# Moving the normalisation stage of the first network one step later in a software-pipelined two-network kernel

## What is computed

```python
h = jnp.maximum(_layernorm(x, axis=-1), 0.0)
x = x + _L0_gnn_ref(h, adj, L0_gnn_W_fc, L0_gnn_W_attn)
h = jnp.maximum(_layernorm(x, axis=-1), 0.0)
x = x + _L1_gnn_ref(h, adj, ...)
```

```python
agg = jnp.einsum('bij,bjd->bid', attn, x)
h = layernorm(x + agg, g1[l], beta1[l])
ff = jax.nn.gelu(h @ W1[l] + b1[l], approximate=False) @ W2[l] + b2[l]
x = layernorm(h + ff, g2[l], beta2[l])
```

## Time and profile before

| | |
|---|---|
| runs, median (lowest to highest) | 2784.17 us (2783.93 to 2784.34) |
| profiled execution, span | 2784.2 us |
| mean granted PE clock over the span | 0.982 of full speed |
| PE busy | 2669.2 us, 96% |
| DVE busy | 2296.3 us, 82% |
| ACT busy | 2147.7 us, 77% |
| POOL busy | 1690.8 us, 61% |
| DMA, share of 16 engines | 22.0% |

### The profile page before, as it was taken

The page is one execution under the profiler, slowest core; times in us unless marked ns, Lnnn a source line. Parts: engine busy times, 40 slices in busy tenths (PEclk is TensorE's granted clock), DMA queues, the critical chain, the costliest instruction groups (busy, mean ns, idle before and its releaser), DMA issues.

```text
span 2784.2 us, 53435 instructions
## 1 busy us (share of the span) xinstructions
PE 2669.2 (96%) x16771; PEld 2393.3 (86%) x16868; DVE 2296.3 (82%) x8507; ACT 2147.7 (77%) x3982; POOL 1690.8 (61%) x2197
## 2 busy tenths in 40 slices
PE   3699999999999999999999999999999999999997
PEld 2588888888888989898988898989888998998997
DVE  6998988888888888888888888888988777777774
ACT  4688888878787878787878788877878777776774
POOL 5556666556766655665676665565766645544655
PEclk7699999999999999999999999999999999999999
DMA  5221322122322121212221212221223111111121
GB/s 177 89 69 54 103 81 85 62 82 66 103 81 77 56 80 45 80 65 92 79 96 53 80 65 77 65 71 57 91 81 99 54 52 52 35 52 52 50 64 53
DMA packets 118590, 203.44 MB, mean 73 GB/s; under 512 B 12800, under 2 KB 85536, under 8 KB 118304
## 3 DMA queue, kind: packets, MB, share of 16 engines
q1 hardware_dynamic: 118304, 199.97, 22.0%
HBM read 116.05 MB, written 83.89 MB: 72 GB/s over the span
## 4 chain that ended last, share of the span: by engine, by line
PE 69%; DVE 14%; POOL 7%; issue 6%; ACT 3%; DMA 0%; DVEq 0%; SPq 0%; POOLq 0%; ACTq 0%
PE bank L603 32%; PE bank L586 26%; PE ps_u L562 5%; DVE st L944 3%; DVE g_lo L970 3%; POOL xo L372 3%; PE ps_u L644 2%; POOL rs L1258 2%; PE ps_s L557 2%; DVE ub L1025 2%; POOL hb L372 1%; DVE ub L1055 1%; PE ps_s L549 1%; DVE ub L939 1%; ACT g_hi L835 1%
## 5 line engine op out<-in xcount | busy, mean ns | idle before, releaser
L603 PE MATMUL bank<-w_hi,g_hi 128*128 128x256 f32 x3072 | 894.1, 291 | 18.7 <-DVE g_lo L970 18.0
L603 PE MATMUL bank<-w_hi,g_lo 128*128 128x256 f32 x3072 | 867.7, 282 | 0.0
L603 PE MATMUL bank<-w_lo,g_hi 128*128 128x256 f32 x3072 | 866.3, 282 | 0.0
L835 ACT ACTIVATE g_hi<-bank,b_eff 128x512 fp32r<-128x512 f32 x768 | 529.1, 689 | 431.9 <-PE bank L586 426.5
L970 DVE TENSOR_TENSOR g_lo<-bank,g_hi 128x512 fp32r<-128x512 f32 x768 | 517.0, 686 | 178.3 <-ACT bank L837 165.2
L586 PE MATMUL bank<-zt_hi,w_hi 128*128 128x512 f32 x1536 | 646.7, 421 | 9.5 <-DVE g_lo L970 4.1
L603 PEld LDWEIGHTS bank<-w_hi,g_hi 128*128 128x128 f32 x3072 | 581.3, 189 | 30.5 <-DVE g_lo L970 29.3
L586 PE MATMUL bank<-zt_hi,w_lo 128*128 128x512 f32 x1536 | 607.2, 395 | 0.0
L586 PE MATMUL bank<-zt_lo,w_hi 128*128 128x512 f32 x1536 | 606.4, 395 | 0.0
L603 PEld LDWEIGHTS bank<-w_lo,g_hi 128*128 128x128 f32 x3072 | 581.7, 189 | 0.8
L603 PEld LDWEIGHTS bank<-w_hi,g_lo 128*128 128x128 f32 x3072 | 581.1, 189 | 0.0
(11 more groups left out here) (98 smaller groups left out, 4235.0 us busy)
## 6 DMA issues: line engine op xcount, KB each, us to landing
xb<-x_scratch SPq DMA_DIRECT2D x88, 512.0 KB, 3.9
x_scratch<-xo SPq DMA_DIRECT2D x64, 512.0 KB, 4.6
xin<-in_x SPq DMA_DIRECT2D x38, 512.0 KB, 5.8
r_scratch<-elu_r SPq DMA_DIRECT2D x32, 512.0 KB, 3.0
xin<-r_scratch SPq DMA_DIRECT2D x32, 512.0 KB, 4.8
out<-xo SPq DMA_DIRECT2D x32, 512.0 KB, 3.2
m<-m_scratch SPq DMA_DIRECT2D x96, 128.0 KB, 3.9
x_scratch<-h SPq DMA_DIRECT2D x24, 512.0 KB, 2.9
```

The costliest lines, as they stand in the source:

```text
L603: mm = pe.matmul(y, g[:, c, r * P:(r + 1) * P], w[:, l, c, :], start=(c == 0 and n == 0), stop=(c == C - 1 and n == 2))
L835: act.activation(g_hi[:, c, :], block_in, ACT.Gelu, bias=bias).then_inc(g_hi_ready, 1)
```

## The change

From group 8 on, stage 3 is done one step later: it leaves the input step, where it stood beside stage 0 of the next group, and goes into the middle step, beside stage 1 of the next group. `input_statistics` goes from behind `g_low(3)` to behind `second_variance`, that is from ahead of `g_low(4)` to ahead of `g_low(7)`. SP's waits for the stored rows of a chunk's last group are put at the load that needs them. Groups 0 to 7, whose steps have another order (L1161 to L1194), stay as they are.

```diff
@@ the stages of a group @@
-        stage_of = {early_step(v) + j: {} for v in range(G) for j in range(4)}
+        def stage_step(v, j):
+
+            return early_step(v) + j + (1 if v >= CH and j == 3 else 0)
+
+        stage_of = {s: {} for s in range(-FILL, U + 2)}
         for v in range(G):
             for j in range(4):
-                stage_of[early_step(v) + j][j] = v
+                stage_of[stage_step(v, j)][j] = v
@@ SyncE @@
                     sp.dma_start(m1[(s + 3) % 2][:, :, :].bitcast(I32), pick(m_u, st, group(s + 3))).then_inc(m_in, 16)
-                    if layer(s + 3) == 0 and group(s + 3) == G - 1:
+                    if s >= PER and layer(s + 3) == 0 and group(s + 3) % CH == CH - 1:
                         sp.wait_ge(h_out, 16 * st.nth0(group(s + 3) - CH))
...
                 if live(s - 2):
-                    if s >= PER and live(s + 4) and layer(s + 4) == 0 and group(s + 4) % CH == CH - 1:
-                        sp.wait_ge(h_out, 16 * st.nth0(group(s + 4) - CH))
                     sp.wait_ge(xo_ready, st.nth(s - 2))
@@ VectorE, the steady step @@
                 first_norm()
                 g_low(3)
-                input_statistics()
                 g_low(4)
                 g_low(5)
                 second_statistics()
                 g_low(6)
                 second_variance()
+                input_statistics()
                 g_low(7)
                 input_variance()
```

## The result

The changed kernel takes 2803.27 us (median of 4 runs, 2801.71 to 2803.68) against 2784.05 us (4 runs) for the kernel before: ratio 1.0067, 95% interval 1.0053 to 1.0080. It is slower by 19 us, where 14 us were forecast.

The account below looks back on a forecast made before the run. PE, busy for 96% of the span, was taken to bound the kernel. Middle steps at +14.6 us and input steps at +0.5 or less gave +14 on 2784.2, so 2798 us, range 2784 to 2810.

Parts of the forecast that it names:

- two gates: Input step: PE held by g_low(7), then by weights for turns, at nearly the same lateness; relieving one alone gives nothing.
- Part 1: Input step: statistics moved ahead of g_low(7) gain 0; the variance of vb takes 0.02 us more, bounds -0.1 and +0.5.
- rival (a): Input steps fall to 26.24 us because earlier chunks 4 to 6 or g_low(7) let PE through; 2773 us, chance 0.10.
- first gate: Input step: L603 matmul waits for DVE's g_low(7), which ends at 1214.55; forecast to stay where it is.
- Part 2: Stage 3 leaving the input step frees 2.00 us of DVE behind g_low(7); the step keeps 27.3 us.
- The earlier start removes this loss of 0.94 us: Middle steps behind last-layer units: POOL's affine part starts at least 2 us earlier, so 27.84 us loses its excess over 26.90.
- Part 3: Middle step: 2.00 us stage 3 block ahead of next_weights against 0.95 us slack; +1.15 us, to 28.05 in the loop.
- rival (b): Stage 3 block costs DVE 1.40 us instead of 2.00, its small operations closing up; 2784 us, chance 0.10.
- covers on POOL and ACT: Later made_root and make_rows stay hidden: POOL had been idle 4.54 us, GELU of step 40 has 0.7 us to spare; cost 0.
- rival (d): Delays reach the late step, ACT's or POOL's cover short by 0.5 us in 23 steps; 2810 us, chance 0.10.
- rival (c): Variance in the input step misses POOL's boundary, +0.5 us in 23 steps; 2810 us, chance 0.06.
- The sum: Middle steps +14.6 us, input steps +0.5 us or less; total +14 on 2784.2 us, giving 2798 us.

Follow-up runs that it names:

- Experiments 4, 5 and 6: Kernel before, with input statistics behind low half of chunk 7 plus spacer copy: 2787.55 us; next_weights ahead of next_dots and made_variance: 2783.94 us; both: 2778.46 us.
- experiment 2: Kernel before with only the input statistics moved, behind the second variance; stage 3 stays in the input step: 2786.77 us, ratio 1.0008.
- experiment 1: Changed kernel with the input statistics put back ahead of g_low(4), so stage 3 alone is moved: 2802.54 us, ratio 1.0062.
- experiment 9: Changed kernel with POOL's last-layer residual added for one graph of four: 2796.85 us, ratio 1.0050.
- Experiment 3: Changed kernel with DVE's next_weights ahead of next_dots and made_variance: 2777.25 us, ratio 0.9971.
- experiment 8: Changed kernel with input statistics behind g_low(7), next_weights ahead of next_dots and made_variance, and ACT's turned copy ahead of make_rows: 2748.95 us, ratio 0.9874.

## Why the prediction was right, and where its size was off

**What bounds the kernel.** Right: two gates of nearly the same lateness in the input step. Experiments 4, 5 and 6 show it as -2.9, +0.5 and +25.5 us in the input steps, against the 25 us that were read from one input and one bare step.

**Part 1, statistics.** Right in sign, and small as forecast: +0.02 us a step against 0.06 measured in experiment 2 (1.4 us over 23 steps) and 0.03 between the changed kernel and experiment 1 (0.7 us). The rival (a), that chunks 4 to 6 being early opens the first gate, fell: `g_low(7)` ends where it did, to 0.06 us.
The variance ended within 0.05 us of the end of an addition of POOL in steps 38 and 39 of the kernel before and, both times, in step 42 of the changed one. By the measured rows the price per meeting is up to 0.59 us (0.76 against 0.17). The Trainium skill ("SBUF — State Buffer", "Who interferes with whom") says that the engine that comes second is blocked until the other's instruction ends. The traces agree for these variances.

**Part 2, stage 3 leaves the input step.** Right that the step keeps its 27.3 us, and that POOL's affine part starts 2 us earlier (1.89 us into step 39 before, 0.29 us ahead of it now). The term that was mis-sized is the one after it: "The earlier start removes this loss of 0.94 us." Only 0.53 us went: step 42 takes 28.46 us, 0.41 more than the 28.05 of a plain middle step. The forecast's own rows did not give the whole: the root at 10.54 us, 2.00 us earlier, is at 8.54, and it was wanted at 8.00. And the forecast saw only a late root, where DVE and POOL also meet. In the kernel before, three small operations of DVE stood beside the four residual additions in step 42 and took 0.70, 0.65 and 0.65 us instead of 0.22, 0.16 and 0.16, each up to the end of an addition to 0.03 us:

```profile
1314.49 2.83 POOL L372 TENSOR_TENSOR xo<-xo,xin 128x256 f32<-128x256 f32 x4 [0.16 <-POOL xo L372]
...
1315.27 0.70 DVE L910 TENSOR_SCALAR small<-dots,ab_col 128x4 f32<-128x4 f32 x1
1316.01 0.65 DVE L912 TENSOR_TENSOR small<-small 128x4 f32<-128x4 f32 x1
1316.69 0.65 DVE L914 SCALAR_TENSOR_TENSOR small<-small 128x4 f32<-128x4 f32 x1
```

They cost DVE 1.5 us there. The root held it by some 0.2 us more (an estimate: `ub` began at 1318.36, 0.83 us behind the start of `g_low(2)`, where 0.61 us lie between them in step 27 of the changed kernel). In the changed kernel the residual runs until 8.38 us into step 42. The three operations are clear of it, but the first variance, due at 7.9, is not, and by way of the second meeting (experiment 9) seven steps lose 0.3 to 0.4 us each, 2.7 us in all.

**Part 3, stage 3 enters the middle step.** Right to a few hundredths: 2.00 us of block, 0.95 us of slack, 0.05 us of restart, 28.05 us in the loop and 27.85 outside. Steps 27, 30, 33, 51, 54 and 57 take 28.03 to 28.06 us, steps 12 and 15 take 27.78 and 27.79. Experiment 3 shows that the order alone makes the wait; the rival (b), a block of 1.40 us, fell with 1.99 measured. The covers on POOL and ACT held, and rival (d) did not come. What rival (c) describes, a variance that misses the end of one of POOL's operations, came in another step: not in the input step (0.27 us there) but in middle steps (up to 0.77 us). The store of the rows has less room than the description of the kernel says: by the code a group's rows are used 5 to 19 steps after they are stored, not 15 to 22, and those of group 15, stored at 892.6 us and loaded at 925.6 before, are now stored at 921.1 and loaded at 927.2, one step later. Step 28 kept its length, 28.41 us, so this cost nothing either.

**The sum.** +14 forecast, +18.5 us measured in the steps; in the middle steps alone 14.6 and 18.4. Of the missing 3.8 us, 2.7 are the residual beside DVE (experiment 9). Steps 24 and 48, the first of the loop's body, are 0.4 and 0.5 us over their forecast and keep it in experiment 9; the second meeting of that experiment is in them too. In step 24 of the changed kernel it went the other way about: the variance of `vb` took 0.27 us, POOL's four additions 3.27 instead of 2.82, and DVE then waited 0.41 us for POOL's root. Steps 36 and 60 are 0.2 us over their kind: DVE is idle for 0.13 us with no semaphore behind it ahead of `g_low(2)`, `hb` comes 0.2 us later, and the variance of `vb` takes 0.59 us instead of 0.37. Steps 39 and 63 are 0.3 us over: DVE is idle for 0.32 us, again with no semaphore (the first DVE row of step 39 shown above), ahead of the weights. The same four steps are as long in the runs of experiments 1 and 9. What these idles are was not tried. Steps 6 and 9, which were taken from step 48 at 27.37 us, had been 27.56 and 27.59, which takes 0.4 us off again.

## What to carry to other kernels

Before work is moved off a step that stalls, list every wait in it that would hold next, each with how late it is: where two are equally late, as here, removing one is worth nothing, removing both is worth all, and only the pair can be judged by a run. Where the work goes, it must stand behind what the bounding engine asks for next: the same 2 us of VectorE work cost 1.1 us a step ahead of the awaited weights and, on the mean, 0.14 us behind them (the 3.3 us of the late steps in experiment 3). And read the slack of the receiving step from each kind of that step, with what the neighbouring engine does at the same time: a delay that an engine has made up for can come back through the engine it feeds.

## What the runs showed of the hardware that was not expected

A VectorE `tensor_scalar` of four columns took 0.17 us alone, and 0.37 (step 39 before), 0.65 and 0.76 us (step 42 of the changed kernel) beside GpSimd's 128x256 additions of about 0.7 us. The two-input operations of four columns met them in the same way: 0.65 instead of 0.16 us (step 42 before). Each ended within 0.03 us of the end of an addition. Where VectorE's small operation got through first, GpSimd paid: 3.27 us for its four additions instead of 2.82 (step 24 of the changed kernel).

At the loop's turn PE stood idle for 1.6 us (before, changed) to 1.9 us (experiment 8) with no semaphore behind it; there it is the largest idle left.
